# Layer 0's entry reordered: spread and gram of group 0 before other preparation, norm factors summed on GpSimd

## What is computed

```python
def hypergraph_conv(x, adj, W, b):
    H = (adj != 0).astype(x.dtype)
    w = adj.reshape(N, -1)[:, :C]            # first row of adj
    xw = jnp.einsum('ncd,hd->nch', x, W)
    Dn = jnp.einsum('nce,ne->nc', H, w)      # degrees
    Dn = jnp.where(Dn > 0, 1.0 / Dn, 0.0)
    Be = 1 / H.sum(axis=1)                   # 0 where the sum is 0
    m = Be[:, :, None] * jnp.einsum('nce,nch->neh', H, xw)
    return Dn[:, :, None] * jnp.einsum('nce,neh->nch', H, m) + b
...
h = jax.nn.relu(hypergraph_conv(x, adj, W1, b1))   # 512 wide
h = layer_norm(h, gamma, beta)
y = hypergraph_conv(h, adj, W2, b2)                # 256 wide
x = _layernorm(x + y + x)
```

## Time and profile before

| | |
|---|---|
| median of 3 runs | 691.17 us (691.11 to 691.23) |
| span of the profiled execution | 689.5 us |
| TensorE busy | 632.2 us, 92% |
| VectorE busy | 565.4 us, 82% |
| ScalarE busy | 527.5 us, 76% |
| GpSimd busy | 372.0 us, 54% |

### The profile page before, as it was taken

How to read it: one execution, slowest core, us unless ns; L and a number is a source line. 1 busy time by engine, 2 the same in 40 slices (tenths; PEclk the granted TensorE clock), 3 DMA queues, 4 the chain that set the end, 5 groups by cost and what they waited for, 6 DMA issues and landing times.

```text
span 689.5 us, 15919 instructions
## 1 busy us (share of the span) xinstructions
PE 632.2 (92%) x5014; PEld 455.5 (66%) x5014; DVE 565.4 (82%) x1744; ACT 527.5 (76%) x1191; POOL 372.0 (54%) x448
## 2 busy tenths in 40 slices
PE   5989999999999999789989699999999997999993
PEld 4667777777777776555656456566666664778783
DVE  3899998888888886778888768988888887578886
ACT  4567878877787887668888667777777775799995
POOL 1235556665555555756656524443434343798883
PEclk9999999999999999999999899999999998999998
DMA  9581439463644322576566324555454543488883
GB/s 276 168 221 47 84 71 226 84 148 94 156 111 105 63 32 47 106 140 136 131 132 138 61 62 87 101 90 98 88 99 87 100 85 63 77 177 181 181 184 124
DMA packets 176771, 80.35 MB, mean 117 GB/s; under 512 B 122416, under 2 KB 174128, under 8 KB 176688
## 3 DMA queue, kind: packets, MB, share of 16 engines
q1 hardware_dynamic: 166512, 70.54, 44.1%
q0 software_dynamic: 8448, 8.39, 8.4%
q10 hardware_dynamic: 1728, 0.40, 0.3%
HBM read 28.97 MB, written 8.39 MB: 54 GB/s over the span
## 4 chain that ended last, share of the span: by engine, by line
PE 31%; DVE 8%; DMA 8%; POOL 7%; issue 4%; ACT 3%; ACTq 0%; POOLq 0%; DVEq 0%
PE banks L86 10%; PE banks L88 9%; PE banks L87 9%; DMA xT_lo<-x_halves 5%; POOL x_halves L1130 3%; DMA l_TT_lo<-l_T_lo 2%; DVE l_st L1044 2%; POOL l_rstd L1069 2%; DVE l_pre L1321 1%; POOL l_U L1976 1%; PE banks L1569 1%; POOL l_T_lo L1773 1%; PE banks L1847 1%; PE banks L1234 1%; ACT x_resident L1078 1%
## 5 line engine op out<-in xcount | busy, mean ns | idle before, releaser
L1078 ACT ACTIVATE x_resident<-l_pre,l_nmr,l_rstd 128x256 f32<-128x256 f32 x256 | 142.1, 606 | 9.4 <-POOL l_nmr L1072 8.9
L973 POOL TENSOR_TENSOR hq<-hq 128x512 f32<-128x512 f32 x48 | 69.4, 1446 | 95.4 <-ACT hq L690 93.2
L1130 POOL TENSOR_TENSOR x_halves<-x_resident,x_halves 128x1024 f16<-128x1024 f32 x46 | 98.1, 2132 | 28.7 <-DVE l_pre L1321 24.6
L1044 DVE BATCH_NORM_STATS2 l_st<-l_pre 128x6 f32<-128x256 f32 x256 | 92.2, 411 | 0.0
L86 PE MATMUL banks<-Wk_lo,xT_hi 128*128 128x258 f16 (+1 forms) x256 | 84.5, 330 | 0.7 <-DVE l_far_lo L1724 0.6
L87 PE MATMUL banks<-Wk_hi,xT_lo 128*128 128x258 f16 (+1 forms) x256 | 84.4, 330 | 0.0
L88 PE MATMUL banks<-Wk_hi,xT_hi 128*128 128x258 f16 (+1 forms) x256 | 84.3, 329 | 0.0
L1069 POOL TENSOR_TENSOR l_rstd<-l_veps,minus_half 128x4 f32<-128x4 f32 x64 | 70.0, 1094 | 15.0 <-DVE l_veps L1058 10.9
L86 PE MATMUL banks<-W2T_lo,h_hi 128*128 128x257 f16 x256 | 71.0, 277 | 5.1 <-ACT zf L702 3.4
L87 PE MATMUL banks<-W2T_hi,h_lo 128*128 128x257 f16 x256 | 70.9, 277 | 0.0
L88 PE MATMUL banks<-W2T_hi,h_hi 128*128 128x257 f16 x256 | 70.9, 277 | 0.0
(11 more groups left out here) (202 smaller groups left out, 1941.2 us busy)
## 6 DMA issues: line engine op xcount, KB each, us to landing
adj<-in_adj SPq DMA_DIRECT2D x32, 256.0 KB, 3.9
x_halves<-in_x SPq DMA_DIRECT2D x16, 512.0 KB, 4.4
x_resident<-b_half SPq DMA_DIRECT2D x8, 1024.0 KB, 7.7
x_resident<-in_x POOLq DMA_DIRECT2D x16, 512.0 KB, 6.1
out<-x_resident SPq DMA_DIRECT2D x15, 512.0 KB, 3.2
l_adjT<-adjT_resident SPq DMA_DIRECT2D x16, 256.0 KB, 2.6
x_resident<-in_L_gnn_W SPq DMA_DIRECT2D x2, 512.0 KB, 5.3
x_resident<-in_L_gnn_Wk SPq DMA_DIRECT2D x1, 768.0 KB, 9.4
```

The source lines that it names most:

```text
L973: pool.tensor_tensor(hq[:, 0, :], hq[:, 0, :], hq[:, h, :], ALU.add).then_inc(hqs_ok, 1)
L1044: dve.bn_stats(L.st[p][:, j, :], L.pre[p][:, j, :]).then_inc(L.st_ok, 1)
L1078: act.activation(K.x[:, gcols(g, j)], L.pre[p][:, j, :], ACT.Identity, bias=L.nmr[p][:, j:j + 1], scale=L.rstd[p][:, j:j + 1]).then_inc(L. ...
L1130: pool.tensor_tensor(F.xs[p][1], x_group(K, g), F.xs[p][0], ALU.subtract).then_inc(F.x_lo, 1)
```

## The change

TensorE's new order is: 18 products of two identity tiles (`first_busy`, results not used), `transpose_adj(0)`, 16 more of them, `degree(0)`, `turn_w1`; `spread(0)`, `turn_w2`, `gram(0)`, `transpose_adj(1)`, `mix_x(0)`, `fold_gamma`; `hidden(0,0)`, `hidden(0,1)`, `degree(1)`, `hidden(0,2)`, `hidden(0,3)`, `spread(1)`, `transpose_adj(2)`, `gram(1)`, `fold_beta`, `turn_qkv`, `project(0,0)` and on as before. W1 is loaded before W2, each with a semaphore of its own.

Both folds become three adds of 128 x 256 on GpSimd (`sum_gamma`, `sum_beta`) and one product by the tile of ones. The gamma sum goes to bank 1, so `gram(1)` waits for the mean to be read. ScalarE scales by beta and halves b2 after the high halves of x, and `high_w2` goes behind relu of `hidden(0,1)`. VectorE's order is: `counts(0)`, both scalings, `operator(0)`, `low_w1`, `mixed_low(0)` twice, `incidence(1)`, `edge_weights(1)`, `centre_w2`; `degrees(1)`, `hidden_low` 0 and 1, `low_w2`, `counts(1)`, both scalings, `hidden_low` 2 and 3, `keep_beta`, `products`, `operator(1)`. Three semaphores of a later layer that nothing uses are dropped.

```diff
@@ loads
-        sp.dma_start(w2n, W2.rearrange("(t p) h -> p t h", p=128)).then_inc(w12_in, 16)
-        sp.dma_start(w1n, W1.rearrange("(t p) d -> p t d", p=128)).then_inc(w12_in, 16)
+        sp.dma_start(w1n, W1.rearrange("(t p) d -> p t d", p=128)).then_inc(w1_in, 16)
+        sp.dma_start(w2n, W2.rearrange("(t p) h -> p t h", p=128)).then_inc(w2_in, 16)
@@ pieces
+    def keep_busy(pe, times):
+        for _ in range(times):
+            pe.matmul(K.bank[7][:, 0:128], K.ident16[:], K.ident16[:], start=True, stop=True)
+
+    def first_busy(pe):
         pe.wait_ge(const, 4)
-        pe.wait_ge(w12_in, 32)
+        keep_busy(pe, 18)
...
-    def fold(pe):
+    def fold_gamma(pe):
         pe.wait_ge(const, 7)
-        pe.wait_ge(w2g_ok, 2)
-        for h in range(HT):
-            m = pe.matmul(K.bank[6][:, 0:D], K.ones[:], w2g[:, h, :], start=h == 0, stop=h == HT - 1)
-        m.then_inc(fold_ps, 1)
-        for h in range(HT):
-            m = pe.matmul(K.bank[7][:, 0:D], K.ones[:], w2b[:, h, :], start=h == 0, stop=h == HT - 1)
-        m.then_inc(fold_ps, 1)
+        pe.wait_ge(g_sum, 3)
+        pe.matmul(K.bank[1][:, 0:D], K.ones[:], w2s[:, 0, :], start=True, stop=True).then_inc(fold_ps, 1)
+
+    def fold_beta(pe):
+        pe.wait_ge(g_sum, 6)
+        pe.matmul(K.bank[7][:, 0:D], K.ones[:], w2s[:, 1, :], start=True, stop=True).then_inc(fold_ps, 1)
+
+    def sum_gamma(pool):
+        pool.wait_ge(w2g_ok, 1)
+        pool.tensor_tensor(w2s[:, 0, :], w2g[:, 0, :], w2g[:, 1, :], ALU.add).then_inc(g_sum, 1)
+        for h in range(2, HT):
+            pool.wait_ge(g_sum, h - 1)
+            pool.tensor_tensor(w2s[:, 0, :], w2s[:, 0, :], w2g[:, h, :], ALU.add).then_inc(g_sum, 1)
...
+            if g == 1:
+                pe.wait_ge(W.mean_ok, 1)
@@ TensorE's step
-            if has(0):
+            if has(0) and g != 1:
                 spread_degrees(g, p)
             if has(-1):
                 hidden(g - 1, q, 1)
+            once(g, 1, degree, 1, 1)
+            if has(-1):
                 hidden(g - 1, q, 2)
...
+            once(g, 1, spread_degrees, 1, 1)
+            once(g, -1, W.first_busy, pe)
+            once(g, 0, W.turn_w2, pe)
+            once(g, 0, gram, 0, 0)
             if has(1):
                 transpose_adj(g + 1, q)
-            if has(0):
+            if has(0) and g != 0:
                 gram(g, p)
+            once(g, -1, W.keep_busy, pe, 16)
...
+            once(g, 1, W.fold_beta, pe)
             once(g, 1, W.turn_qkv, pe)
...
-            once(g, 0, W.fold, pe)
+            once(g, 0, W.fold_gamma, pe)
...
-            once(g, -1, W.turn_w12, pe)
+            once(g, -1, W.turn_w1, pe)
@@ ScalarE's step
-            once(g, 0, W.high_w2, act)
+            once(g, 0, W.scale_beta, act)
+            once(g, 0, W.halve_b2, act)
...
+            once(g, 0, W.high_w2, act)
+            if has(0):
                 square(g, 0)
...
-            once(g, -1, W.halve_b2, act)
@@ GpSimd's step
             once(g, -2, W.constants, pool)
+            once(g, -2, W.sum_gamma, pool)
             once(g, -2, W.sum_rows, pool)
+            once(g, -2, W.sum_beta, pool)
```

More of the change, by code:

```diff
@@ L272, in turn_w12, with turn_w2 @@
         m.then_inc(wT_ps, 1)
+    def turn_w2(pe):
+        pe.wait_ge(w2_in, 16)
         for h in range(HT):
@@ L363, in centre_w2 @@
         dve.wait_ge(fold_ps, 1)
[L364 removed]
+        dve.tensor_scalar(mean, K.bank[1][:, 0:D], 1.0 / H, None, ALU.mult).then_inc(mean_ok, 1)
         dve.wait_ge(mean_ok, 1)
@@ L367, in centre_w2, with keep_beta @@
             dve.tensor_tensor(w2c[:, h, 0:D], w2g[:, h, :], mean, ALU.subtract).then_inc(w2c_ok, 1)
+    def keep_beta(dve):
         dve.wait_ge(fold_ps, 2)
@@ L405, in setup @@
     W.sync = sync
-    W.turn_w12, W.fold, W.turn_qkv = turn_w12, fold, turn_qkv
+    W.turn_w1, W.turn_w2, W.turn_qkv = turn_w1, turn_w2, turn_qkv
+    W.first_busy, W.keep_busy = first_busy, keep_busy
+    W.fold_gamma, W.fold_beta, W.sum_gamma, W.sum_beta = fold_gamma, fold_beta, sum_gamma, sum_beta
+    W.scale_beta, W.keep_beta = scale_beta, keep_beta
     W.vectors, W.high_w1, W.scale_w2, W.high_w2 = vectors, high_w1, scale_w2, high_w2
@@ L657, in step @@
                 mix_x(g, p, 1)
-            once(g, 0, W.fold, pe)
+            once(g, 0, W.fold_gamma, pe)
             if has(-1):
                 project(g - 1, 2)
-            if has(1):
+            if has(1) and g != 0:
                 degree(g + 1, q)
-            once(g, -1, W.turn_w12, pe)
+            once(g, -1, W.turn_w1, pe)
             if has(-1):
@@ L890, in step @@
             q = 1 - p
-            if has(1):
+            once(g, 0, degrees, 1)
+            if has(1) and g != 0:
                 counts(g + 1, q)
@@ L900, in step @@
                 normalise(g - 1, q, 3)
-            if has(1):
+            if has(1) and g != 0:
                 scale_incidence(g + 1, q, 1)
-            once(g, -1, W.low_w1, dve)
             if has(0):
@@ L906, in step @@
                 hidden_low(g, 1)
+            once(g, 0, W.low_w2, dve)
+            once(g, 0, counts, 1, 1)
+            once(g, 0, scale_incidence, 1, 1, 0)
+            once(g, 0, scale_incidence, 1, 1, 1)
+            if has(0):
                 hidden_low(g, 2)
@@ L911, in step @@
                 hidden_low(g, 3)
+            once(g, 0, W.keep_beta, dve)
             once(g, 0, W.products, dve, 0)
@@ L933, in step @@
             once(g, 3, W.score_columns, dve)
-            if has(1):
+            if has(1) and g >= 0:
                 mixed_low(g + 1, q, 0)
@@ L937, in step @@
                 norm_variance(L, dve, g - 1, q, 0.25 * EPS)
-            if has(1):
+            if has(1) and g >= 0:
                 mixed_low(g + 1, q, 1)
             once(g, -1, W.centre_w2, dve)
-            if has(2):
+            if has(2) and g != -1:
                 degrees(g + 2)
-            once(g, -1, W.low_w2, dve)
             once(g, 0, W.low_qkv, dve)
@@ L1402, in attention_front @@
     S = Parts()
-    S.s_ps, S.s_hi, S.s_lo, S.s_bias, S.sj_ps, S.t_ok, S.e_ok, S.u_ok = (
+    S.s_bias, S.sj_ps, S.t_ok, S.e_ok, S.u_ok = (
         ctx.enter_context(nc.semaphore(f"l{layer}_{name}"))
-        for name in ("s_ps", "s_hi", "s_lo", "s_bias", "sj_ps", "t_ok", "e_ok", "u_ok"))
+        for name in ("s_bias", "sj_ps", "t_ok", "e_ok", "u_ok"))
+    if layer == 3:
+        S.s_ps, S.s_hi, S.s_lo = (ctx.enter_context(nc.semaphore(f"l3_{name}")) for name in ("s_ps", "s_hi", "s_lo"))
     S.s = [ctx.enter_context(nc.sbuf_tensor(f"l{layer}_s_{s}", [128, GP], F16)) for s in ("hi", "lo")]
```

19 lines of the change are left out of this document (16 added, 3 removed).

## The result

The changed kernel takes 693.42 us (median of 22 executions, 691.29 to 697.39), the kernel before in the same comparison 691.60 (22 executions, 689.23 to 694.27): ratio 1.0027, with an interval of 1.0016 to 1.0038. That is slower by 1.8 us where the prediction had 4.0 us faster; 693.42 lies outside its range. The profiled execution has a span of 691.3 us and a time of 693.05; before it was 689.5.

A forecast was written before the change was run, and what follows sets the result against it. TensorE was taken to bound the kernel, so an earlier layer 0 body moves everything; -2.26 (gram) - 1.23 (mix_x) - 2.5 (fold and degree) + 1.0 (high_w2) + 1.0 (clock) = -4.0, 691.17 to 687.2 us, range 685.7 to 689.4.

The forecast's parts named there:

- Steps 1 to 4: Entry up to hidden(0,0): busy products free, gram(0) 2.26 us earlier, mix_x(0) 1.23 shorter, fold out of the way; 6.0 us earlier.
- step 1: Start of the entry: 18 and 16 busy products and W1 loaded first cost zero, by a few tenths.
- The early fall of the clock: Rival: clock falls already before mix_x(0), gram costs 0.4 and mix_x 1.23 us more, 688.9 us; chance 0.17.
- Step 5: ScalarE behind hidden(0,1): high_w2 gives back 1.0 us, centre_w2 ends at 20.4, copy_degrees(1) runs at 22.4; 5.0 us left.
- Step 6: From copy_degrees(1) to mix_x(1): old order and its 8.0 us to operator(1) stay, mix_x(1) at 31.2, 5.0 us saved.
- the fill's lateness: GpSimd's add_x(0) waiting for the fill DMA: up to 0.6 us lost, taken as zero.
- Step 7: TensorE around gram(1): a nearly empty stretch makes the clock fall, costing 1.0 us (0.6 to 1.3); mix_x(1) at 32.2.
- The first paragraph: Layer 0's body, 60 to 240 us, is TensorE-bound; starting it earlier moves everything behind it by the same amount.
- The slower rival: Low clock lasts beyond one stretch, group 1 at half speed, each further stretch costs 1.71 us, 693.0 with four; chance 0.05.
- The sign: Whole kernel: faster, meaning under 689.8 us, with chance 0.87; slower with 0.05.

The follow-up runs named there:

- early_counts: The changed kernel with VectorE's counts(1) and both scalings moved ahead of hidden_low(0); 694.31 us against 691.87 for the kernel before.
- late_sums: The changed kernel with GpSimd's add_x(0) first and group 0's sums behind VectorE's four h_lo; 691.62 us against 691.44 for the kernel before.
- no_busy: The changed kernel without the 18 and 16 busy identity products at the start; 692.38 us against 691.87 for the kernel before.
- joined: GpSimd's order of late_sums with TensorE's program of level_fill; 688.15 us against 691.44 for the kernel before, ratio 0.9942.
- level_fill: no_busy with 12 products of 512 columns in front of gram(1), restoring TensorE's old instruction count; 692.20 us against 691.44 for the kernel before.
- fill40: The changed kernel with 40 identity products on TensorE in front of gram(1); 693.28 us against 691.87 for the kernel before.
- pad_before: The kernel before with 86 satisfied waits (43 instructions) on TensorE ahead of the first transposes; 694.62 us against 692.13.
- joined_off: joined with 42 more TensorE instructions, 21 identity products while it waits for adj(0); 691.01 us against 692.06 for the kernel before.
- tiny21: The kernel before with 21 one-column products (42 instructions) on TensorE ahead of adj(0); 692.78 us against 691.05.
- after: The changed kernel itself, in its first profiled execution; median 693.42 us against 691.60 for the kernel before.
- level_after: no_busy with 24 instructions of satisfied waits on TensorE, restoring the old instruction count; 693.17 us against 692.13 for the kernel before.
- late_vector: The kernel before with four memsets on VectorE ahead of group 0's first mixed_low; 690.88 us against 692.13.
- tiny64: The kernel before with 64 one-column products (128 instructions) on TensorE ahead of adj(0); 694.04 us against 691.05.
- before_late: The kernel before with 45 identity products in front of hidden(0,0); 699.19 us against 691.87.

## Why the prediction was wrong, by its own steps

- *Steps 1 to 4 right for the entry, step 1 wrong behind it.* Gram(0) 11.26 (11.35 said), mix_x(0) 12.76 for 2.02 (12.84, 2.02), hidden(0,0) 16.24 (16.25). The early fall of the clock, a rival with 0.17, isn't in either trace of the changed kernel, but it is in two kernels with its entry (early_counts, late_sums): in single executions it happens. For the entry the products of step 1 were rightly priced at nothing, and no_busy shows that they were worth nothing. For the rest of the kernel "cost zero" was wrong: they are the reason that TensorE's stream is longer at all (43 instructions more with them, 24 fewer without), and in the traces layer 2 loses 2.17 and 2.76 us with them and 0.25 without.
- *Step 5 right:* the centre ended at 20.03 beside GpSimd (20.4 said), the copy of the degrees started at 22.36.
- *Step 6 failed.* It took VectorE's 6.1 us and the 8.0 us to operator(1) over from before as they stood. But there GpSimd's sums had begun at 29.73, behind VectorE's scaling and its first two h_lo (timelines of both engines before, below); 5 us earlier they fall on incB_hi (1.74 for 0.69) and on h_lo (3.35 for 1.29). I had worked out in step 5 that the two engines exclude each other, and didn't apply it to the work that moved together. The Trainium skill (SBUF — State Buffer, "Who interferes with whom") puts it as an exclusive lock on the shared ports; the traces agree, down to P, which reads PSUM and took 0.68 beside the sums in late_sums. late_sums and joined show it as the cause: with the sums behind h_lo both scalings are back at 0.69 and 0.68 and the two h_lo at 1.29 together, mix_x(1) comes at 30.47 in joined, and joined is 4.0 us faster than level_fill. Step 6 also took the fill's lateness as nothing: GpSimd waited 1.07 us for it in the first trace and 0.47 in the second. The shorter wait went with the longer h_lo (4.41 against 3.35 us), so it isn't this wait that cost the gain.

```profile
26.29 0.69 DVE L814 TENSOR_TENSOR incB_hi<-incT,rcs_hi 128x512 f16<-128x512 f16 x1
26.90 0.68 DVE L814 TENSOR_TENSOR incB_lo<-incT,rcs_lo 128x512 f16<-128x512 f16 x1
27.50 1.29 DVE L839 TENSOR_TENSOR h_lo<-hf,h_hi 128x512 f16<-128x512 f32 x2
```

```profile
29.73 1.32 POOL L973 TENSOR_TENSOR hq<-hq 128x512 f32<-128x512 f32 x1 [17.10 <-ACT hq L690]
```

- *Step 7 right in kind, small in size.* The clock fell at 24.90. fill40 without it hands over 0.5 us earlier; 1.0 was taken.
- *The first paragraph failed*: "what starts that body earlier moves all behind it by the same amount". Through layer 0 it is so (-2.37 at 60, -2.39 at 291 us). But the change puts 43 more instructions into TensorE's stream ahead of the later layers, and 42 or 43 of them cost 2.5 us by the medians in pad_before, 2.9 in joined_off and 1.7 in tiny21. No step priced the length of the program, and no rival had it.
- *The sum as it was:* handover -1.7 to -2.4 instead of -4.0, packets +2.2 to +2.8 in layer 2; in the two traces the rest up to 680 us is +1.4 (mostly the seam) and +0.2, and 0.6 more come behind 680. Together +1.8 and +1.9, the difference of the spans. The two traces place this rest differently. Part of it goes with the clock: the executions of the changed kernel had a mean granted clock of 0.978 (the second set 0.979), those of before 0.983 to 0.984, and within the changed kernel's executions 0.001 of it goes with 0.46 us. By that slope the 0.005 to 0.006 between the two kernels would be an estimated 2.3 to 2.8 us, more than the whole difference; but part of it is the entry's low stretch, which is in the handover already, and part the seam's. How much of the 1.8 us is due to the clock isn't separated. It can't be the loss in layer 2, where the clock falls in no trace.
- *The sign.* The slower rival (0.05) was the clock staying low. It was another thing.

## What to carry to other kernels

When two engines exclude each other, list every pair of instructions that a move brings side by side, not only the new ones; and put a sum that is not urgent behind the other engine's urgent pieces by a wait. If a tight kernel loses some us far from the edit, look at the packets of the instruction queue beside the late transfers, and test it by a few idle instructions in front: if 43 instructions that do nothing move the time as much as the change does, the change was not judged yet. joined and joined_off differ by 42 such instructions and by 2.9 us at the median, of which their traces show 1.3 in layer 2. And where traces are to explain a difference of 2 us, see first where the traced execution stands among its like.

## What the runs showed of the hardware

- TensorE's instructions arrive in 16 KB packets, which the profile lists among those of the core's DMA engines (q8, 41 packets); such a packet beside a transposing DMA (xT_lo) makes 3.1 us into 3.6 at the median and up to 4.95, the more the later it starts in the transfer.
- A VectorE multiplication of two f16 tiles in SBUF (128x512, 0.69 us) took 1.74 to 3.16 us beside GpSimd's sums.
- A satisfied wait isn't free on TensorE: 86 of them, two to an instruction, took from 1.92 to 6.68 us (pad_before), 0.055 us each, and held its first transposes back from 4.30 to 6.68.
- Where the clock falls varies between executions of one kernel. Where a low stretch of 3.4 us starts between 296.6 and 301.6, at the start of layer 1, 1.0 to 1.7 us are lost from 291 to 303 us (after, level_after, late_vector, level_fill, joined, tiny64); where it starts between 277.9 and 284.0, nothing is. Where one starts at 359.6 or 363.8 (tiny21, before_late), 1.3 us are lost from 303 to 405.
